# Second experts of a two-layer AdaLN kernel: the first weight matrix becomes the stationary operand and is fetched tile by tile

## What is computed

```
def _L1_ffn_ref(hidden_states, Wr, br, W1, W2):      # E = 8, H = 256, FFN = 1024
    x = hidden_states.reshape(-1, h)
    route = jax.nn.sigmoid(x @ Wr + br)
    max_prob = jnp.max(route, axis=1, keepdims=True)
    max_ind = jnp.argmax(route, axis=1)
    for e in range(8):
        mask = (max_ind == e)[:, None]
        y = jax.nn.gelu(x @ W1[e], approximate=False) @ W2[e]
        out = out + mask * y
    return out * max_prob
```

## Time and profile before

| | us |
|---|---|
| median of 3 runs (lowest to highest) | 1907.46 (1904.87 to 1910.49) |
| the profiled execution's own time | 1909.01 |
| its span in the profile | 1907.3 |
| router stage, from the last attention work to the last store issued | about 1546 to 1589 |
| routing | about 1590 to 1609 |
| second experts | about 1611 to 1865 |
| combine and stores of the result | about 1867 to 1907 |

### The profile page before, as it was taken

The page is one execution under the profiler, slowest core; times in us unless marked ns, Lnnn a source line. Parts: engine busy times, 40 slices in busy tenths (PEclk is TensorE's granted clock), DMA queues, the critical chain, the costliest instruction groups (busy, mean ns, idle before and its releaser), DMA issues.

```text
span 1907.3 us, 35939 instructions
## 1 busy us (share of the span) xinstructions
PE 1628.7 (85%) x12648; PEld 1156.5 (61%) x12648; DVE 1180.0 (62%) x1808; ACT 876.0 (46%) x1928; POOL 1077.4 (56%) x910
## 2 busy tenths in 40 slices
PE   6799999977899999999999368788878765999991
PEld 5455555565788888888888233244434253777771
DVE  7789899975333333333444686999999985212224
ACT  6644444343444444444544275444434353444443
POOL 5568777632333333333543698999988953232322
PEclk9899999975899999999999678999989885999996
DMA  5013332127233333333432410011102354111115
GB/s 200 23 48 108 111 111 96 38 68 287 99 97 101 100 101 101 101 101 95 167 111 63 160 45 1 23 30 30 29 26 72 138 168 164 40 42 44 42 37 182
DMA packets 115013, 171.49 MB, mean 90 GB/s; under 512 B 28112, under 2 KB 78304, under 8 KB 114720
## 3 DMA queue, kind: packets, MB, share of 16 engines
q1 hardware_dynamic: 104384, 140.61, 22.4%
q0 software_dynamic: 10464, 28.59, 4.6%
HBM read 105.58 MB, written 63.57 MB: 89 GB/s over the span
## 4 chain that ended last, share of the span: by engine, by line
PE 60%; DVE 13%; POOL 12%; issue 5%; DMA 3%; ACT 2%; SPq 0%; DVEq 0%; POOLq 0%; ACTq 0%
PE ps L685 56%; POOL BIG L2138 10%; DVE BIG L1231 7%; DVE BIG L1686 2%; PE ps L1017 2%; DMA HB<-BIG 1%; ACT BIG L1737 1%; DMA BIG<-YT 1%; DVE X L1231 1%; POOL BIG L2320 1%; PE ps L927 1%; POOL X L2138 1%; PE ps L799 1%; DVE bnst L1238 0%; PE ps L999 0%
## 5 line engine op out<-in xcount | busy, mean ns | idle before, releaser
L685 PE MATMUL ps<-BIG 128*128 128x256 f16 (+8 forms) x9868 | 1288.5, 305 | 131.9 <-DVE BIG L1664 43.5
L685 PEld LDWEIGHTS ps<-BIG 128*128 128x128 f16 (+3 forms) x9868 | 904.4, 101 | 455.0 <-issue 85.1
L2138 POOL TENSOR_TENSOR BIG<-BIG 128x512 f16<-128x512 f32 (+6 forms) x547 | 776.3, 1451 | 436.0 <-ACT BIG L1737 414.4
L1231 DVE TENSOR_TENSOR BIG<-ps,BIG 128x512 f32<-128x512 f32 (+3 forms) x559 | 376.9, 732 | 245.5 <-ACT BIG L1737 202.3
L1737 ACT ACTIVATE BIG<-ps 128x64 f32<-128x64 f32 (+7 forms) x877 | 323.3, 428 | 348.9 <-PE ps L685 239.9
L1737 ACT ACTIVATE BIG<-BIG 128x512 f16<-128x512 f32 (+4 forms) x465 | 284.8, 627 | 300.8 <-DVE BIG L1231 266.4
L1231 DVE TENSOR_TENSOR BIG<-BIG 128x512 f16<-128x512 f32 (+11 forms) x256 | 219.3, 867 | 110.8 <-ACT BIG L1737 105.0
L1231 DVE TENSOR_TENSOR BIG<-BIG,ps 128x512 f32<-128x512 f32 (+2 forms) x212 | 124.8, 592 | 257.7 <-PE ps L685 241.5
L2276 POOL DMA_INDIRECT YT<-BIG x109 | 108.7, 998 | 266.7 <-ACT BIG L1737 266.1
L1686 DVE TENSOR_REDUCE BIG<-BIG 128x160 f32<-128x2560 f32 x64 | 182.3, 2848 | 0.0
L2270 POOL DMA_INDIRECT BIG<-HB,BIG x109 | 108.4, 994 | 71.0 <-DVE BIG L1231 39.7
(11 more groups left out here) (132 smaller groups left out, 950.6 us busy)
## 6 DMA issues: line engine op xcount, KB each, us to landing
WD<-BIG SPq DMA_DIRECT2D x112, 256.0 KB, 2.5
BIG<-in_v SPq DMA_DIRECT2D x32, 512.0 KB, 4.3
BIG<-WD SPq DMA_DIRECT2D x32, 512.0 KB, 5.2
BIG<-in_w SPq DMA_DIRECT2D x24, 512.0 KB, 3.9
BIG<-WD SPq DMA_DIRECT2D x32, 384.0 KB, 8.0
BIG<-YT SPq DMA_DIRECT2D x24, 512.0 KB, 4.8
HB<-BIG SPq DMA_DIRECT2D x64, 128.0 KB, 2.1
BIG<-OW SPq DMA_DIRECT2D x32, 128.0 KB, 2.1
```

Source lines behind the costliest of these rows:

```text
L685: return e.matmul(o, lhsT, rhs, start=start, stop=stop, skip_group_check=True)
L1231: return e.tensor_tensor(o, a, b, op)
L2138: return e.tensor_tensor(o, a, b, op)
```

## The change

1. **First weights**: the first matrices' halves are stored in a DRAM tensor of their own, `WG`, in which the row of 8 KB for (expert, partition) holds both halves. They are no longer brought on chip as a whole. For each tile POOL issues one indexed gather (`fetch_weights`) of 128 rows of 8 KB, 1 MB, into a fixed ring of three (`W1`).
2. **Order of operands**: in `up` the weight block of 128 x 128 is stationary and the 128 rows of the tile stream. A tile has 48 matmuls of 128 columns in place of 12 of 512. Inner features come out on partitions, so `turn_up` is gone. ACT takes the high half and DVE the low half out of the GELU's output on chip; `UPT` becomes a ring of two.
3. **Second weights** only are held on chip: 16 pieces of 512 KB in place of 32. The lists of pieces shrink from 4, 7, 2, 6 and 13 to 4, 4, 2, 4 and 2.
4. **Routing**: in the second layer the expert of each tile is computed between the one-hot steps u = 1 and u = 2, with two more DVE operations that form the row numbers `wi` of `WG`.
5. Some DMA semaphores are shared in another way (`ld_mw`), which moves no instruction.

```diff
             def up(j, hf):
...
+                    pe.wait_ge(ld_u[j % 3], 16 * (j // 3 + 1))
                     pe.wait_ge(s["hTc"], at(l, "hTc") + j + 1)
-                    for k in range(2):
-                        for p, (a, b) in enumerate(HALVES):
-                            m = mm(ps[(2 * j + hf) % 4][:, :], m_.HTT[j % 2][:, 2 * a + k, :],
-                                   weight(l, j, b, 1024 * k + 512 * hf, 512), k == 0 and p == 0, k == 1 and p == 2)
+                    w = shaped(m_.W1[j % 3], (2, 2, 1024))
+                    for blk in range(4):
+                        for k in range(2):
+                            for p, (a, b) in enumerate(HALVES):
+                                f = 512 * hf + 128 * blk
+                                m = mm(ps[(2 * j + hf) % 4][:, 128 * blk:128 * blk + 128], w[:, a, k, f:f + 128], m_.HTT[j % 2][:, 2 * b + k, :],
+                                       blk == 0 and k == 0 and p == 0, k == 1 and p == 2)
...
                     up(j, 0)
-                    if j:
-                        turn_up(j - 1)
                     up(j, 1)
...
-            late = [7, 10, 18, 21, 22, 23, 24, 25, 26, 27, 28, 30, 31]
+            late = [7, 10]
             for n in range(3, NT):
                 rows_out(1, n)
-                if n % 4 == 3:
+                if n % 4 == 3 and late:
                     weights_in(1, late.pop(0))
-            for i in late:
-                weights_in(1, i)
...
+            def fetch_weights(j):
+                m_ = M[1]
+                pool.wait_ge(s["rt"], rt_at[1, "wi"])
+                if j >= 3:
+                    pool.wait_ge(s["up_ps"], at(1, "up_ps") + 2 * (j - 2))
+                e.indirect_dma_start(m_.W1[j % 3], None, WG, bass.IndirectOffsetOnAxis(m_.wi[:, j:j + 1], 0)).then_inc(ld_u[j % 3], 16)
...
+                fetch_weights(0)
                 for r in range(4):
                     pool.wait_ge(st_hb[r], slot_base[1]["hb"] + 128)
                 fetch(1, 0)
                 fetch(1, 1)
-                for j in range(M[1].NS):
-                    if j + 2 < M[1].NS:
+                fetch_weights(1)
+                for j in range(NS):
+                    if j + 2 < NS:
+                        fetch_weights(j + 2)
                         fetch(1, j + 2)
                     if j:
                         put(1, j - 1)
```

More of the change, by code:

```diff
@@ L224, in __init__ @@
                 self.nslab = 3 if gated else 2
-                self.span = 2 * self.nslab * 2048
+                self.span, self.pieces = (2 * 2048, 16) if l else (2 * self.nslab * 2048, 32)
                 self.HB = dram(f"HB{l}", [T, 2 * D], f16)
@@ L228, in __init__ @@
                 NS = self.NS
-                area = Area(E * self.span // 2)
+                area = Area(32768 if l else E * self.span // 2)
                 self.SLs = area(CH, NT)
@@ L268, in __init__ @@
                 self.UP = area.ring(2, 1024 if l else 512)
-                self.UPT = area.pairs(1 if l else 2, 8, self.rows)
+                if l:
+                    behind = Area(E * self.span // 2)
+                    self.W1 = behind.ring(3, 4096, dt=f16)
+                self.UPT = (behind if l else area).pairs(2, 8, self.rows)
                 self.YO = area.ring(2, D)
@@ L520, in convert_store @@
                 x, n, src, k, hf = M[l].slabs[c]
+                if l:
+                    for m in range(2):
+                        to = 2048 * m + 1024 * hf
+                        e.dma_start(WD[1][:, 4096 * x + to:4096 * x + to + 1024] if n else WG[128 * x:128 * x + 128, to:to + 1024],
+                                    pr[m]).then_inc(st_cv[c % 2], 16)
+                    return
                 for m in range(2):
@@ L537, in weights_in @@
             def weights_in(l, i):
-                n = M[l].E * M[l].span // 32
+                n = M[l].E * M[l].span // M[l].pieces
                 for k in range(2):
@@ L639, in sync @@
                     sp.wait_ge(s["fin"], 12)
-                    for i in (4, 5, 16, 17, 29, 8, 11):
+                    for i in (4, 5, 8, 11):
                         weights_in(1, i)
@@ L648, in sync @@
             sp.wait_ge(s["pm"], pm_p[NQ - 1])
-            for i in (12, 13, 14, 15, 19, 20):
+            for i in (12, 13, 14, 15):
                 weights_in(1, i)
@@ L697, in mod_columns @@
                 pe.wait_ge(s["cT"], 1)
-                pe.wait_ge(ld_m[part], 16)
+                pe.wait_ge(ld_mw[part], 16)
                 if part:
@@ L1502, in routing, with experts_of_groups @@
                     dve.wait_ge(s["hT"], at(l, "hT") + NT)
+                def experts_of_groups():
+                    n = c.next()
+                    tt(m_.cmp, bc(m_.ends, 1, m_.NG), bc(m_.it_g, 2, E), ALU.is_le).then_inc(n, 1)
+                    n = c.next()
+                    e.tensor_reduce(m_.ex, m_.cmp, AX.X, ALU.add).then_inc(n, 1)
+                    n = c.next()
+                    e.tensor_scalar(m_.ex, m_.ex, float(E - 1), float(m_.span), ALU.min, ALU.mult).then_inc(n, 1)
+                    n = c.next()
+                    e.tensor_copy(m_.ei, m_.ex).then_inc(n, 1)
+                    rt_at[l, "ei"] = c.n
+                    if l:
+                        dve.wait_ge(s["konst"], KONST)
+                        n = c.next()
+                        e.scalar_tensor_tensor(out=m_.it_g, in0=m_.ex, scalar=128.0 / m_.span, in1=pcol[:, 0:1].broadcast_to([128, m_.NG]),
+                                               op0=ALU.mult, op1=ALU.add).then_inc(n, 1)
+                        n = c.next()
+                        e.tensor_copy(m_.wi, m_.it_g).then_inc(n, 1)
+                        rt_at[l, "wi"] = c.n
                 for u in range(4 * CH):
+                    if l and u == 2:
+                        experts_of_groups()
                     ch, g = u // 4, 8 * (u % 4)
@@ L2306, in second_experts @@
                         put(1, j - 1)
-                put(1, M[1].NS - 1)
+                put(1, NS - 1)
             def combine(i):
```

101 lines of the change are left out of this document (37 added, 64 removed).

## The result

The changed kernel took **1874.11 us** (1872.92 to 1876.34, 4 runs) against 1907.72 for the kernel before (4 runs): a ratio of **0.9825** (0.9807 to 0.9843). The forecast was 1875, range 1869 to 1893. The time was hit.

A forecast was written before the change was run, and what follows sets the result against it. The second experts were taken as bound by PE's matmul stream. Tiles -30.4, router -4.0 and routing +1.4 sum to -33.0 us, from the median 1907.46 to 1874.5, so 1875 us, range 1869 to 1893.

The forecast's parts named there:

- Tiles on PE, -0.78 us each: Second experts: without transposes, and with weight loads hidden at 0.056 us per matmul, a tile takes 5.53 us against 6.31.
- times 39 = -30.4: Second experts: the saving of 0.78 us per tile on PE, taken over all 39 tiles, gives -30.4 us.
- Queue order: POOL's queue, second experts: rows gathered behind weights land at 7.5 to 8.3 us, needed at 8.2; fits or misses by 0.1.
- Rival (a): Second experts: rows land late behind the weights and `turn` waits; kernel around 1885 us; chance 0.19.
- POOL, bytes, ACT: Second experts, per tile: POOL 3.8 us, bytes 3.2 to 4.2, ACT near 3.1, all hidden under PE's 5.53.
- DVE: covered: Second experts: DVE takes 1.9 us per tile; the 2.2 us path of GELU and halves hides behind a tile's work.
- (b): Second experts: POOL becomes the bound through slow gathers of 8 KB rows; 2075 us at the high bound; chance 0.08.
- (c): Second experts: DMA bytes become the bound at 208 GB/s, 6.3 us per tile; kernel 1905 us; chance 0.06.
- (d): `up` on PE: weight loads not hidden in a long stream, 0.098 us per pair; kernel 1953 us; chance 0.04.
- Router, -4.0: Router stage: without weight pieces between row stores, ACT's two store waits go; -4.0 us, between -3.0 and -4.7.
- Routing, +1.4: Routing of the second layer: computing the experts earlier delays the one-hot steps; +1.4 us, between +0.5 and +1.8.
- Attention, nothing: Attention: the weight pieces missing there cost and gain nothing, since nothing in that stage waits for them.

The follow-up runs named there:

- e_router: Kernel before with only the router's part: late weight pieces from between the row stores moved behind the last row tile; 1902.12 us, ratio 0.9984.
- b2_again: The kernel before, unaltered, run again; 1904.82 us, ratio 0.9993.
- e_on_chip: Kernel before with the operands of `up` swapped alone, weights read on chip by register address, no fetch; 1936.57 us, ratio 1.0168.
- e_turn_early: Changed kernel with `turn` of the next tile between the halves of `up`, and POOL fetching rows ahead of weights; 1872.54 us, ratio 0.9837.

## Why the prediction was right, and where it was not

- **Tiles on PE, -0.78 us each: right.** The transposes are gone, a matmul with its own load takes 0.056 us also in a stream of 48, and the tile is 5.52 us. The 81 ns of the Trainium skill ("TensorE: Matmul & The Clock Gate", section "Back-to-back issue gap") and the 1921 us that would follow are not what this kernel shows; rows 5 were the better guide.
- **"times 39 = -30.4": wrong in the sum.** It needs that nothing is ever late. The second experts gained 18.8 in the first measurement, 31.9 without the weight gathers (254.1 to 222.2). Of the 11.6 us that are missing, 9.9 are waits for rows. The step that failed is "so it fits, or misses by 0.1" in *Queue order*: rows came up to 1.7 us too late, so, counted by its estimate, they landed as late as 9.9 us after the end of `down(j - 1)` where 7.5 to 8.3 was the estimate and 8.2 the need. Rival (a) had the right mechanism and was given 0.19; it happened in 11 tiles of 38 and cost 9.9 us. POOL issued the rows at +3.3 (median), as estimated (3.4); what I had too short is the time from issue to landing. I had built it from medians, and a margin of nothing should be read as "late in some tiles".
- **POOL, bytes, ACT: right. DVE: covered, but read from the wrong row.** A weight gather takes 0.971 us (0.97 forecast); 359 GB/s lies in 316 to 410; ACT's high half takes 0.63; DVE's low half takes 0.69 where I had 0.93. The 0.93 of rows 7 is the mean of 140 operations of the first experts; in the second experts DVE's low half took 0.686 before, with its source in PSUM, so taking it out of on-chip memory changed nothing. Rivals (b), (c) and (d) fell.
- **Router, -4.0: right in kind, too large.** The stage lost 2.7 us, and `e_router` alone about 3. ACT's two waits of 2.67 and 2.04 became 0.56 and 1.14, so 3.0 was to be had. I had given back 0.7 for what is late next; the bare ring of stores keeps 1.7. And the gain is not there in every execution: in three of the ten with the change the stage took 53.3 to 54.0, as without it.
- **Routing, +1.4: right** (+1.6).
- **Attention, nothing: right**, as far as repeats can tell (378.8 to 384.1 with, 379.0 to 383.3 without).
- **Not seen: the merge, -2.9 us, and the end, -6.1 us.** With them the sum came out right for the wrong reason: -19.9 from the terms that I had, -9.0 from two that I had not, and -7.2 from two stages where I had nothing, of which the 4.2 us of the attention are chance and the 3.0 ahead of the merge at most in part the change.
- **Not seen: the late signal.** That the path of GELU, high half and low half is covered was true of `down`. But the next tile's `up` waits for ACT's copy of the turned rows, and this copy stands behind that same GELU and behind `turn`'s own signal, which is late too. From GELU to the next `up` it takes 0.49 + 0.74 = 1.23 us (1696.35, 1696.84, 1697.58 above). The cover is `turn` and `down`, 2.94 us from the end of `up` (1693.84 to 1696.78). That leaves 1.7 us of slack; a signal 2.5 us late overdraws it by 0.8, which is what PE waits. About half of it is ACT's order and half `turn`'s late signal (the estimate above). I had costed ACT by its busy time and asked for the slack of one consumer only.

**The two changed stages.** In the merge the same 32 additions of POOL and 32 scaled additions of DVE are shorter, before and after:

```profile
L2138 POOL TENSOR_TENSOR X<-X,BIG 128x256 f32<-128x256 f32 x32 | 24.5, 766 | 3.0 <-DVE BIG L1231 2.9
L1620 DVE SCALAR_TENSOR_TENSOR BIG<-BIG 128x256 f32<-128x256 f32 x32 | 24.1, 753 | 14.0 <-POOL BIG L2320 14.0
```

```profile
L2142 POOL TENSOR_TENSOR X<-X,BIG 128x256 f32<-128x256 f32 x32 | 21.8, 680 | 2.2 <-DVE BIG L1223 2.1
L1628 DVE SCALAR_TENSOR_TENSOR BIG<-BIG 128x256 f32<-128x256 f32 x32 | 21.8, 680 | 14.4 <-POOL BIG L2338 14.4
```

POOL's took 766 to 779 ns in three executions without the fetch and 678 to 686 in four with it. It is not fewer bytes beside them: the DMA queues moved 9.63 MB in this stage before and after. In the first stage, too, POOL's 58 operations of 1024 columns take 2.06 us each with the change and 2.14 without (four executions of each). The change also moves tiles to other places on chip; whether that shortens the operations was not tried.

At the end, the last instruction of POOL is a DRAIN, before and after, and SP's branch shows when the other engines were done:

```profile
L73 POOLq DRAIN  x1: 9908/9908/9908, 1897.1 to 1897.1; - x1
L73 SPq COMPARE_BRANCH  x1: 38/38/38, 1900.7 to 1900.7; - x1
```

```profile
L73 POOLq DRAIN  x1: 2645/2645/2645, 1867.1 to 1867.1; - x1
L73 SPq COMPARE_BRANCH  x1: 38/38/38, 1870.8 to 1870.8; - x1
```

Before, everything had ended at 1900.9 and the kernel waited until 1907.0 for POOL alone.

**What stays open** is why the signals are late in some measurements. What is shown: it is those of the second half of `up` and of `turn` behind it, not that of the first half (but for the very first tile, in three runs); with the weight gathers the late signal of `up` comes 1.6 to 2.5 us after its end in the median of a run, without them 1.0; neither the bytes nor `down`'s address computations decide. It needs the dense stream of the new `up` as well: on the same chips no GELU is late in `b2_again`, `e_router` and `e_on_chip`, where the matmuls of `up` are fewer or come only each 0.15 us. And it goes with the chip or with the hour: no chip was measured twice, so the two can't be told apart. One more thing goes with it: in the traces of chips 14, 7 and 0, of the kernel before too, 72 to 148 signals of engines have no record; in those of the first measurement and of chip 9 it is 2 to 5. Of the landing signals of DMAs, 10,500 to 11,100 in a run, 1981 to 2832 have none there, and 25 to 101 here. So something there that records or carries signals may have been short of room. The Trainium skill, "NOTIFIC — the notification-queue block", section "Overflow: three behaviours, one of which stalls the engine", says that a full queue of records either loses records or stalls the engine that makes them. That would fit both signs, but it is an argument. Records are missing in `b2_again` and `e_on_chip` too, where no signal is late; no run here shows a full queue; and whether the kernel would be slow there without a profiler was not tried.

## What to carry to other kernels

Ask of each instruction in an engine's order who waits for what stands behind it, not only for its own result: `turn` moved ahead of the second half made the kernel insensitive to a signal 2.9 us late. That is one line moved on PE, one on ACT, and one on POOL for the rows. Where a transfer is needed sooner than another, it goes first on the queue; a landing computed to within 0.1 us of its need was late here in 11 of 38 tiles. And measure a change of 2% more than once, on more than one chip: here two of four measurements show 1.7% and two 0.3 to 0.4%, while `e_turn_early` kept its 1.6% on a chip where the changed kernel lost it.

## What was new about the hardware

- A signal from PE can reach ACT 1.0 to 2.9 us after the matmul's end, in some measurements and not in others, for the same program, while PE's own matmuls go on at their usual distance. Two signals of PE, 0.22 us apart by their matmuls' ends, then arrive 0.06 us apart. The Trainium skill, "Perfetto Trace Analysis", section "Per-engine timelines", says that a matmul's end in a profile is estimated, and that its signal leaves only once PSUM has acknowledged all bytes. By that a small gap is normal, and 0.04 us is what the undisturbed traces show.
- POOL's final DRAIN took 9.91 us in each of the four kernels without weight gathers, 2.64 to 2.65 in nine with them, and 8.28 in the one with three weight gathers. It can set the end of the kernel, by 6 us here. What it waits for is open.
- With an address computed in PE's sequencer for each, a long stream of matmuls comes one each 0.15 us in place of 0.056 (`e_on_chip`: 48 computations a tile, tile 7.2 us).
- A gather of 128 rows costs POOL 0.97 us whether a row is 1 KB or 8 KB.
